# Reassociating the product across chunks in a Mamba-style mixer, and starting the first expert inside the last routing

## The reference

```python
x = emb[tokens] * 16 + pos_enc                          # 16 x 256 x 256
h = softmax((x w_q)(x w_k)^T / 16, axis=1) @ (x w_v)    # attention, normalised over queries

z, xBC, dt = split(layernorm(layernorm(h)) @ in_proj.T) # mixer: 512, 768, 8 columns
xBC = silu(conv4(xBC)); xs, B, C = split(xBC)           # 512, 128, 128
# 8 heads of 64, two chunks of 128 tokens; L = exp(segsum(dt * A))
Y_diag = (C B^T * L) @ (xs * dt)                        # inside each chunk
state  = B_0^T @ (decay_0 * xs * dt)                    # what chunk 0 leaves behind
Y_off  = (C_1 @ state) * exp(cumsum(dt * A))            # what chunk 1 gets from it
y = (Y_diag + Y_off + D * xs) * silu(z)
h = h + layernorm(h) + rmsnorm(y) @ out_proj.T

scores = softmax(layernorm(h) @ w_router)               # 8 experts, the best 2 of each token
# a token's place in its expert is its rank among the tokens before it; 1024 places per expert
slot = expert * 1024 + rank, dropped where rank >= 1024
y_e = gelu(x_e @ w1[e]) @ w2[e]                         # 1024 rows per expert, 256 -> 1024 -> 256
out = h + bias; out[token] += weight * y_e[slot]
```

## Time and profile before

| | |
|---|---|
| median of the runs | 920.77 us |
| the profiled execution's own time | 918.74 us |
| its span | 917.0 us |
| PE busy | 98% of the span |
| DVE, ACT, POOL busy | 69%, 58%, 55% |
| mean granted TensorE clock | 1.00 of full speed |
| the chain that ended last | PE 91%, DVE 4%, the rest 1% each |

### The profile page before, as it was taken

The page is one execution under the profiler, slowest core; times in us unless marked ns, Lnnn a source line. Parts: engine busy times, 40 slices in busy tenths (PEclk is TensorE's granted clock), DMA queues, the critical chain, the costliest instruction groups (busy, mean ns, idle before and its releaser), DMA issues.

```text
span 917.0 us, 17798 instructions
## 1 busy us (share of the span) xinstructions
PE 902.9 (98%) x5843; PEld 804.9 (88%) x5843; DVE 629.5 (69%) x1698; ACT 529.1 (58%) x1103; POOL 505.5 (55%) x492
## 2 busy tenths in 40 slices
PE   8999999999999999999999999999999999999998
PEld 7888888888888888898888789999999999999997
DVE  2587889889988898898889644636464646464642
ACT  1766777677777776777677454444444434343442
POOL 5656877887788779777775312232323232223253
PEclk9999999999999999999999999999999999999999
DMA  7940111001000000000000053434343343433221
GB/s 216 324 152 13 36 47 35 23 35 34 13 23 14 24 13 20 17 20 18 13 14 4 27 172 91 110 72 112 73 99 85 85 98 75 109 71 67 24 59 46
DMA packets 49398, 59.13 MB, mean 64 GB/s; under 512 B 6304, under 2 KB 44683, under 8 KB 49360
## 3 DMA queue, kind: packets, MB, share of 16 engines
q1 hardware_dynamic: 35920, 42.14, 14.3%
q0 software_dynamic: 13440, 16.50, 10.5%
HBM read 33.62 MB, written 30.67 MB: 70 GB/s over the span
## 4 chain that ended last, share of the span: by engine, by line
PE 91%; DVE 4%; POOL 1%; issue 1%; ACT 1%; DMA 1%; SPq 0%; POOLq 0%; DVEq 0%
PE bank L1876 13%; PE bank L1877 13%; PE bank L1878 13%; PE bank L1584 11%; PE bank L1727 6%; PE bank L1529 5%; PE bank L1695 5%; PE bank L1653 3%; PE bank L1568 3%; PE bank L1559 3%; PE bank L1550 3%; PE bank L1543 3%; PE bank L1888 1%; PE bank L1748 1%; PE bank L1593 1%; DVE xc L1138 1%
## 5 line engine op out<-in xcount | busy, mean ns | idle before, releaser
L699 POOL DMA_INDIRECT out<-ye,tok_slot x56 | 95.3, 1701 | 249.2 <-DMA out<-ye,tok_slot 128.0
L985 ACT ACTIVATE hf<-bank 128x512 f32<-128x512 f32 x128 | 79.4, 620 | 186.3 <-PE bank L1878 185.7
L1460 DVE TENSOR_TENSOR h_lo<-hf,h_hi 128x512 fp32r<-128x512 f32 x128 | 88.6, 693 | 102.3 <-ACT h_hi L987 102.3
L1876 PE MATMUL bank<-w_hi,h_hi 128*128 128x256 f32 x512 | 146.1, 285 | 0.0
L1878 PE MATMUL bank<-w_hi,h_lo 128*128 128x256 f32 x512 | 144.9, 283 | 0.0
L1877 PE MATMUL bank<-w_lo,h_hi 128*128 128x256 f32 x512 | 144.9, 283 | 0.0
L1138 DVE SCALAR_TENSOR_TENSOR xc<-bank,cw,xc 128x253 f32<-128x253 f32 (+2 forms) x288 | 128.1, 468 | 1.5
L1876 PE MATMUL bank<-xe_hi,w_hi 128*128 128x512 f32 x256 | 99.9, 390 | 0.0
L1877 PE MATMUL bank<-xe_lo,w_hi 128*128 128x512 f32 x256 | 99.8, 390 | 0.0
L1878 PE MATMUL bank<-xe_hi,w_lo 128*128 128x512 f32 x256 | 99.7, 389 | 0.0
L1877 PEld LDWEIGHTS bank<-w_lo,h_hi 128*128 128x128 f32 x512 | 98.3, 192 | 0.0
(11 more groups left out here) (237 smaller groups left out, 2358.7 us busy)
## 6 DMA issues: line engine op xcount, KB each, us to landing
w_raw<-w SPq DMA_DIRECT2D x16, 1024.0 KB, 7.7
slots_dram<-zero_row SPq DMA_DIRECT2D x1, 8320.0 KB, 30.8
xe<-slots_dram SPq DMA_DIRECT2D x15, 520.0 KB, 4.6
out<-hb SPq DMA_DIRECT2D x16, 256.0 KB, 2.1
w_raw<-in_wT SPq DMA_DIRECT2D x2, 644.0 KB, 5.5
out<-zero_row SPq DMA_DIRECT2D x1, 1024.0 KB, 32.5
slots_dram<-rows,slot POOLq DMA_INDIRECT x64, 2.2
out<-ye,tok_slot POOLq DMA_INDIRECT x64, 3.7
```

Of the source, the lines that this page charges most:

```text
L699: g.indirect_dma_start(out, bass.IndirectOffsetOnAxis(ap=tok_slot[q][:, j:j + 1], axis=0), ye[q][:, j, :], None, compute_op=ALU.add).then_ ...
L985: sc.activation(hf[m % 2][:, :], h_bank[i % H_BANKS][:, :], ACT.Gelu_apprx_tanh)\
L1460: vc.tensor_tensor(h_lo[:, m, :], hf[m % 2][:, :], h_hi[:, m, :].bitcast(F32), ALU.subtract)\
L1876: te.matmul(out_, hi, rhi, start=first_, stop=False)
```

## The change

Four things are changed.

1. **Bracketing.** Instead of B_0^T, PE's `state_inputs` makes the product of C_1 and B_0 (128x128), ACT copies that (tile across), and one `across_chunks` in `chunk_state`'s place makes its product with xdec. `chunk_state`, ACT's `state` and `from_state` are gone. Half turn 16 had this bracketing already.
2. **Order in the loop.** DVE's `query_max` and `mask_scores` come ahead of the residual's lm and lv (`residual_moments`), which move from the end of a half turn into the next. DVE's `mask_scores` waits for PE directly, and ACT's copy waits for DVE's mask. `carried_y`, `first_y` and `split_hT` come ahead of `router_top`; on PE `choices_before` moves behind the first third of `project_channels`. POOL's `skip_x` waits for `decay_scores` of chunk 1.
3. **Slots of the last two batches** are counted from the end of each expert's places (`last_slots_of`), so that the first 512 rows of each expert are complete once batch 13 has been scattered.
4. **Expert 0's first 512 rows** are loaded during half turn 16, and their first product is made in half turn 17, between the pieces of the last routing; `keep_clock` is gone from half turn 17 and after. Expert 0's weights are split in half turns 14 and 15 (w2: two pieces of 512 columns in each, on ACT and DVE) and 16 and 17 (w1). For this the expert buffers are cut finer and laid over buffers of part one that are free by then, and SP's stores of the last residuals are put behind or ahead of the new load. The loop over experts begins at group 1 and ends one group later.

The core of the diff:

```diff
@@ sync
+            for p in range(2):
+                sp.wait_ge(scattered[p], 64 * (PAIRS - 1))
+            sp.wait_ge(z_psum[1], z_psum.now(Turn(PAIRS), 1))
+            sp.wait_ge(s_dump, 16)
+            sp.dma_start(xe[0][:, 0:4, :], slots_dram[0:GW, :].rearrange("(j p) c -> p j c", p=P))\
+                .then_inc(xe_loaded[0][0], 16)
+            store_rows(Turn(PAIRS - 1), 1)
@@ gpsimd, half
                 if b:
+                    pool.wait_ge(m_ready[KD - 1][q], m_ready[KD - 1].now(b, q))
                     skip_x(b, q, 0)
                     skip_x(b, q, 1)
@@ scalar
             def state_inputs(r, p):
-                act.wait_ge(btg_psum[p], btg_psum.now(r, p))
-                sc.activation(bs[p][:, :], bank[p][3][:, 0:NS], ACT.Copy)
+                act.wait_ge(gm_ready[p], gm_ready.now(r, p))
+                sc.activation(across[p][:, :], bank[p][3][:, 0:P], ACT.Copy)
...
                 if not f:
+                    hidden(1, 0)
+                    norm_2(t, p)
+                    hidden(1, 1)
+                    transposed_rows(t, p)
+                    hidden(1, 2)
+                    sc.activation(warm[:, :], warm[:, :], ACT.Exp)
+                    router_exp(t, p)
+                    for i in range(3, KF):
+                        hidden(1, i)
+                    return
...
-                if b:
-                    state(b, q)
@@ vector, half
                 if not f:
+                    split_h(1, 0)
+                    last_slots_of(Turn(PAIRS), q)
+                    first_w1_low(1, 3)
+                    first_w1_low(3, 4)
+                    split_h(1, 1)
+                    router_in(t, p)
+                    split_h(1, 2)
+                    router_top(t, p)
+                    describe_rows(t, p)
+                    last_slots_of(t, p)
+                    with_bias(t, p)
+                    split_h(1, 3)
+                    first_slot_infos()
+                    for i in range(4, KF):
+                        split_h(1, i)
+                    return
                 if f:
                     query_max(f, p)
+                if final:
+                    for m in (2 * p, 2 * p + 1):
+                        first_w2_low(m)
                 if b:
                     mask_scores(b, q, q)
+                if f and t:
+                    residual_moments(t, p)
...
+                if b:
+                    carried_y(b, q, bank[q][3])
+                    first_y(b, q)
+                if f:
+                    split_hT(f, p)
                 if t:
                     router_top(t, p)
                 if b:
-                    first_y(b, q)
-                    carried_y(b, q, bank[q][2])
-                if f:
-                    split_hT(f, p)
-                if b:
                     second_y(b, q)
@@ tensor, half
                 if not f:
-                    keep_clock(p, LAST["first"])
-                    choices_before(t, q)
...
+                    pe.wait_ge(first_low, 1)
+                    pe.wait_ge(xe_split, 2)
+                    hidden(1, 0)
+                    hidden(1, 1)
+                    pe.wait_ge(h2_ready[p], h2_ready.now(t, p))
+                    hidden(1, 2)
+                    last_choices_before(t, q)
+                    to_v2T(t, p)
+                    pe.wait_ge(pos_taken[q], pos_taken.now(t, q))
+                    hidden(1, 3)
+                    route(t, p)
+                    pe.wait_ge(w1_split, 1)
+                    hidden(1, 4)
+                    hidden(1, 5)
+                    last_choices_before(t, p)
+                    hidden(1, 6)
+                    hidden(1, 7)
...
                 if b:
                     segment_sums(b, q, 3)
-                    chunk_state(b, q)
+                    across_chunks(b, q, bank[q][3])
                     own_chunk(b, q, 0)
...
-                    from_state(b, q)
                     own_chunk(b, q, 1)
-                if t:
-                    choices_before(t, p)
...
                     project_channels(f, p, 0)
+                if t:
+                    choices_before(t, p)
```

More of the change, by code:

```diff
@@ L285, in lm_block @@
-        unfilled = [eb(f"unfilled{q}", [P, JS]) for q in range(2)]
+        hf = [eb(f"hf{g}", [P, GW]) for g in range(2)]
+        ye_0 = one("ye", [P, JS, DM])
+        w_hi = [[first_w1_hi, first_w2_hi], [eb(f"w{n}_hi1", [P, KD * FF], F32R) for n in (1, 2)]]
+        w_lo = [[first_w1_lo, first_w2_lo], [eb(f"w{n}_lo1", [P, KD * FF], F32R) for n in (1, 2)]]
+        xe = two(xe_0, "xe", [P, JS, ROW])
+        xe_hi = two(xe_hi_0, "xe_hi", [P, KD, GW], F32R)
+        xe_lo = two(xe_lo_0, "xe_lo", [P, KD, GW], F32R)
@@ L380, in run_experts, with groups @@
             turn(NE // 2, True)
+        def groups(last):
+            return range(1, 2 * NG + (0 if last else 1))
         def bc(ap, shape):
@@ L392, in lm_block @@
         DRAIN = dict(rows=2)
-        LAST = dict(first=9, v2T=2, route=2, choices=9)
+        DRAIN_YT = (3, 2)
         PER_TURN = 2 * NG * KF
-        h_bank = bank[0]
+        h_bank = [bank[0][i] for i in (1, 2, 0, 3)]
         x_bank = bank[1][0:2]
@@ L1454, in split_x, with weigh @@
                     ins.then_inc(xe_split, 1)
[L1456 to L1465 removed]
+                def weigh(g, ns=range(4)):
+                    q, half = g // NG % 2, g % NG
+                    for n in ns:
                         if half == NG - 1 and n >= 2 and not (last and q):
```

432 lines of the change are left out of this document (241 added, 191 removed).

## The result

| | before | after |
|---|---|---|
| median of the runs, us | 920.91 | 931.71 |
| lowest to highest | 920.69 to 921.79 | 930.45 to 933.17 |
| ratio of the times, with 95% interval | | 1.0116 (1.0097 to 1.0135) |
| the profiled execution's own time | 918.74 | 930.82 |
| its span | 917.0 | 929.1 |

What follows compares the result with a forecast made beforehand. A ring of waits through DVE, POOL, ACT and PE was taken to set the loop, so shortening PE gained 0. 918.74 + 0 - 10.9 = 907.8, plus 2.03 for the median: 909.9, say 910 us; range 900 to 917.

Steps and rivals of the forecast that it cites:

- from the bn_stats behind it to the end of ACT's hn pass 4.02: Loop, DVE to ACT: this stretch was taken at 4.02 us from the old kernel's rows (386.14 to 390.16).
- the sum of the ring: Loop: waits through DVE, POOL, ACT and PE add to 30.69 us, with handovers some 30.8, today's half turn.
- second_root would start when it did: Loop, POOL: lm and lv come 0.9 us later, but DVE no longer stands still 1.26 us, so second_root's start hardly moves.
- the pair on which my sum rested: Loop: POOL's seg_lo holds DVE's first multiplication by seg until it ends, as skip_x did (0.77 us of hold).
- rival C: Loop: router_top or first y held by POOL's second skip_x, 1.0 us lost per half turn, 924 us; chance 0.09.
- no gain: Loop: bracketing and reordering priced at 0, though PE alone would be 0.75 us shorter per half turn.
- Half turns 14 to 16: End of part one: w2's pieces 2.5 us, turning expert 0's rows 0.8, PE's waiting decay sums 1.5; 4.8 late.
- the second 1.25, 0.8 and 1.5: Half turns 15 and 16: two w2 pieces on DVE 1.25 us, PE's turning of rows 0.8, waiting decay sums 1.5.
- The seam: Half turn 17: blocks start at 524.9, second group's first product at 553.0 instead of 563.89, gain 10.9 us.
- rival B: Seam: PE's standstill brings 1.2 GHz for three blocks, or second-product waits reach their upper bound; 4 us lost, 914; chance 0.13.
- the waits for h_lo: Half turn 17, second product: the first quarter waits for h_lo and takes 5.3 us, between 2.9 and 8.
- D: Experts: expert 1's weights or expert 0's second rows late, or SP's stores in the way; 6 to 10 back, 918; chance 0.08.

## Why the prediction was wrong

**The step that failed** is the term "from the bn_stats behind it to the end of ACT's hn pass 4.02" in the sum of the ring, taken over from the old kernel as if it couldn't change. Term by term, in the changed kernel from half turn 12 into 13, and in the same kernel with the multiplication waiting for shift from 11 into 12 (starts of rows; ends of ACT's are start and duration; at a clock of 1.00 in both):

| term | predicted | changed kernel | with the wait for shift |
|---|---|---|---|
| msq to the end of seg_lo | 10.69 | 11.01 (384.87 to 395.88) | 10.77 |
| rest of the first multiplication | 1.14 | 1.04 | 1.04 |
| bn_stats to the end of hn | 4.02 | 4.89 (396.92 to 401.81) | 4.02 |
| end of hn to hT_lo (transposes and hT, with what stands between) | 2.58 | 2.71 | 3.03 |
| hT_lo | 0.60 | 0.61 | 0.60 |
| router_top | 1.39 | 1.49 | 1.47 |
| second_y to msq | 10.27 | 10.18 | 10.23 |
| sum | 30.69 | 31.93 | 31.16 |

0.87 of the 1.24 is shift, held by the second multiplication: taking the hold away brought this term back to 4.02. 0.32 is POOL, which waits for lv now that maximum and mask stand ahead of it; I had argued that second_root would start when it did. A smaller slip of the sum: it leaves out the stretch between the end of hn and PE's transposes (390.16 to 390.71), because PE's own product fills it. With the hold it's gone (0.05), without it 0.33 of it are back, which is most of what is left over 30.69 there.

**What was right there.** The ring, not PE, sets the half turn: bracketing alone gained nothing, and the multiplication by seg waits for seg_lo. That a POOL instruction and a DVE one hold each other is borne out in both directions, 1.88 for 1.22 on DVE and 1.07 for 0.20 on POOL, but I applied it only to the pair on which my sum rested. (The Trainium skill, "SBUF — State Buffer", section "Who interferes with whom", says that a DVE instruction with two SBUF inputs and a GpSimd one that reads SBUF keep each other out for the whole instruction. The trace agrees: shift, 0.20 us by itself, takes 1.07 and ends at 400.75, 0.06 behind the multiplication.) The rival C was of this kind, and its 1.0 per half turn is near the 1.1 measured, but it had another pair: router_top or the first y held by skip_x. The range of 900 to 917 left it out. The rows of before held a warning besides hu_s: the 1.26 us at lv, read as DVE standing still, are a 2-column instruction that ends with POOL's hb (409.88 to 411.14), and takes 0.16 where nothing runs beside it.

Why the order of the two turned can be read from the rows, though no run isolates it. shift comes 1.42 or 1.43 us behind lnv in both kernels. Before, DVE's lmax had to wait for PE's router logits, 0.27 us behind lnv, and the second multiplication came 1.47 behind lnv; now DVE comes later, the logits are there, lmax follows at 0.07, and the multiplication comes at 1.21. The hold of the first multiplication (1.88 for 1.23), which I used for "no gain", is one thing that makes DVE late, but not the only one: with w2's pieces behind the scaling of v in the old order, half turn 14 has the first multiplication at 1.21 us and shift held all the same (1.07). The margin of 0.04 us could be read from the rows of before.

**Half turns 14 to 16.** Predicted 4.8, measured 10.2 (7.5 and 2.8). The pieces of w2 were priced as DVE's work, and that part was right: in half turn 14 the way from msq to the end of seg_lo is 12.30 us against 11.01. The fall of the clock behind PE's waits wasn't priced at all. The three stretches of 4 us at 0.66, 0.50 and 0.56 lack 5.1 us of full clock (an estimate from these rows), and in the kernel that waits for shift the spare products, with which the clock stayed at 1.00, took half turn 14 from 39.58 to 33.01. From half turn 15 to the route 2.8 came against 3.6 (the second 1.25, 0.8 and 1.5); PE's waits for seg_lo there are 0.58 and 0.83. Moving the pieces made it no better.

**The seam.** The idle stretch was foreseen (3 us, 3.14), and in the kernel with the old order the first block stands at 525.90 against a forecast of 524.9. That it comes so near is partly luck: 1.7 us of it are the fall of the clock in half turn 13, which nobody priced. From the route to the second group the gain was 11.4 instead of 15.7 (32.2 us forecast, 36.5 measured). Of the 4.3 missing, 1.6 came in the eight blocks (14.9 against 13.3) by the lower clock, which rival B had. The other 2.7 came in the first three quarters of the second product (13.8 against 11.1). There the waits for h_lo, 2.5 us, were as forecast; the granted clock was 0.88 over these 13.8 us, which makes 1.6. The remaining 1.1 are open.

**The rest.** The loads of rows and weights were in time, so D didn't happen; 1.9 came behind the seam, against none forecast.

What stays open is why the clock falls in one half turn and not in the next with the same waits. Since the profiles of two kernels can differ by such a fall that no edit brought about, differences of 2 us and less between the kernels with the changed end are not shown by one profile.

## What to carry to other kernels

Before summing a ring of waits from old rows, list for each short instruction in it what the other engine starts within a microsecond around it: an order that holds by 0.04 us is no property of the kernel, and a 0.2 us instruction can cost 0.9 when it falls on the wrong side. Then try the change in parts: here one part was free, one lost 14 us and one gained 7, and the sum hid all three. A wait put in by hand (0.5 to 0.8 us here) can be cheaper than a hold. And a gain in one stretch is only a gain once the stretch behind it has been looked at: the 2.4 us of the blocks were lost again in the second product.

## What the runs showed of the hardware that I had not expected

- The granted clock falls to 1.2 GHz behind waits that are short against PE's work. It fell behind 0.61 and 0.50 us around one row of products of 1.97, and in other half turns of the same kernel with the same two waits it did not. It stayed low for 3 to 17 us, and in the loop such a fall cost 1.0 to 1.7 us.
- Behind 3.14 us of standing still, eight blocks of products took 15.8 us (14.9 in the changed kernel), and 13.4 where spare products filled the stretch. Behind 2.21 us the clock fell in one kernel and not in the next.
- A product of 128 columns takes 0.23 us, a transposition of as many 0.11.
- Two kernels with the same work and the same order but for two small POOL instructions (hu_s and shift) lie 2.3% apart (1.0016 and 1.0242 of before).
